# Feature buffer laid out feature by feature, and ten and nine features looked up instead of eight and seven

## Chip, cores and metric

The kernel runs on one core of one Trainium2 chip. Its time is device microseconds of one launch; the median of three runs stands below. Everything is float32.

## The reference

A recommendation model for 2048 examples: 26 embedding rows of 128 numbers are looked up for each, all pairs of the 27 vectors (26 features and the dense one) are multiplied, and a network of three layers runs on the result.

```python
e = jnp.stack([tbl_0[ids[:, 0]], ..., tbl_25[ids[:, 25]]], axis=1)      # (2048, 26, 128)
sd = jnp.einsum('bfd,bd->bf', e, dense)
ss = jnp.einsum('bfd,bgd->bfg', e, e)
z = jnp.concatenate([dense, sd, ss[:, iu, ju]], axis=1)                 # pairs iu < ju
h = jnp.concatenate([z, dense], axis=1)
h = jnp.maximum(h @ W_top1 + b_top1, 0.0)                               # 607 x 512
h = jnp.maximum(h @ W_top2 + b_top2, 0.0)                               # 512 x 256
y = h @ W_top3                                                          # 256 x 1
```

Ten of the tables have 1000 rows, which is the smallest size; the others have 1250, 12500 or 125000.

## The kernel before

The examples are worked on in eight chunks of 256, numbered by `(h, par)`, chunk `2h + par`. A feature reaches `feat`, the buffer [128 numbers, chunk parity, ...] from which the dot products are made, in one of two ways.

*Gathered.* GpSimd issues two indirect DMAs for a feature and chunk (L374), 128 rows each, into `rows`. TensorE transposes them through `tr_ps` (L573), ScalarE copies the result to `feat` (L412). Features go in units of two or one; the buffer of a unit is free for the next chunk when its transposes are done (`transposed`).

*Looked up.* For the first eight (`par` 0) or seven (`par` 1) of the small tables, the whole table lies in SBUF as a high and a low part. VectorE compares the ids of the chunk with the row numbers (eight comparisons a feature, L515), and TensorE multiplies the two parts with the result (16 matmuls, L588, into `oh_ps`); ScalarE copies to `feat` (L418). At the start each table is loaded by SyncE, split by ScalarE (`table_hi`, L391) and VectorE (`table_lo`, L502).

The dot products of a chunk come in eight steps of 8 groups (L606): each matmul takes one position of the chunk, two examples at once, and two of them run on the two halves of the array's columns. In `feat`, laid out `[QS, Q, FS]`, the 27 features of an example stand side by side, padded to 32. So TensorE reads neighbouring numbers, 59 for the weights and 52 for the moving side, and ScalarE writes feature by feature, 512 bytes apart. ScalarE (L427) and VectorE (L525) copy the products to `dots`, SyncE stores them to DRAM (L288) and loads them again in another order as `zt` (L299, L302). Layer 1 is L628, layer 2 L639, layer 3 L647.

A float32 matmul stands as two instructions in the profile, so a chunk has 256 matmul rows at L606.

The order on TensorE and ScalarE is written out by hand. In `SLOT`, `d` is a step of dot products of the finished chunk, `i` a shift of ids, `r` a unit of transposes of the next chunk, `l` a lookup, `f` the copy of the dense features, `m` a step of the network (`m0` to `m3` layer 1, `m4` layer 2, `m5` layer 3). One slot is run for each chunk. In the last slots, layers of the last two chunks are put behind the last transposes and dot products:

```python
SLOT_BEFORE_LAST = SLOT[0].replace(" m4", "").replace(" m5", "")
SLOT_LAST = "r0 d0 r1 d1 r2 d2 r3 d3 r4 d4 r5 d5 r6 d6 f r7 d7"
...
run("m4 r8 m5 r9", rows=(last, 1), done=(last - 1, 1))
run(DOTS, done=(last, 1))
run(MLP, done=(last, 0))
run(MLP, done=(last, 1))
```

Of the kernel before, what the change touches and what calls it, by code (L numbers as in the profile page):

```python
# [8 lines left out]
N1, N2 = 512, 256  # L9
# [4 lines left out]
LOOKUPS = (8, 7)  # L14
# [18 lines left out]
def units(fs):  # L33
# [8 lines left out]
FS = 32  # L42
# [60 lines left out]
def dlrm_tower(nc, dense_t, idx, ids_t, tables, w1, b1, w2, b2, w3, y):  # L103
    fp32, fp32r, i32 = mybir.dt.float32, mybir.dt.float32r, mybir.dt.int32
# [5 lines left out]
    with ctx:  # L110
# [9 lines left out]
        feat = sb("feat", [P, 2, QS, Q, FS], fp32)  # L120
# [3 lines left out]
        ids_bc = sb("ids_bc", [P, NO, CH], i32)  # L124
        rows = sb("rows", [P, NR, TILES, D], fp32)
        dense_sb = sb("dense_sb", [P, CH], fp32)
# [9 lines left out]
        h2 = sb("h2", [P, CH], fp32)  # L136
# [4 lines left out]
        ids_local = ids_bc[:].bitcast(fp32)  # L141
# [6 lines left out]
        feat1 = feat[:, 1].rearrange("p g q f -> p (g q f)")  # L148

        def raw_table(u):  # L150
            if u == 0:
                return dots[:, 0:RPP * D]
            if u == NO - 1:
                return zt[:].rearrange("p c b -> p (c b)")
            return feat1[:, (u - 1) * RPP * D:u * RPP * D]
# [568 lines left out]
```

## Time and profile before

| | |
|---|---|
| median of three runs | 423.53 us (423.44 to 424.53) |
| the profiled execution | 424.92 us |
| its span, first to last instruction | 422.8 us |
| TensorE matmul busy | 344.4 us (81%) |
| ScalarE busy | 198.8 us (47%) |
| VectorE busy | 163.0 us (39%) |
| GpSimd busy | 288.1 us (68%) |
| TensorE's granted clock, mean | 0.91 of full speed |

Busy times come from the profiled execution, and shares are of its span. TensorE's busy time is in wall time: at half clock the same work counts double. A timeline row merges like instructions that follow one another: start, length from the first start to the last end, number, and in brackets the idle time before them with what ended it. Instructions of TensorE overlap, so the step from one start to the next is what a burst costs, and not its own length. L numbers are lines of the kernel.

### The profile page before, as it was taken

The numbers are of one execution on the slowest core, as the hardware profiler recorded it, in microseconds if no ns is written. First come the engines' busy times: TensorE is split into PE (matmuls) and PEld (weight loads), VectorE is DVE, ScalarE is ACT, GpSimd is POOL, SyncE is SP. The second block draws the span as 40 slices with busy tenths as digits, with TensorE's granted clock in tenths as the row PEclk, the third lists the DMA queues.
The fourth block names the chain that finished last, engine by engine and source line by source line (L and its number), as shares of the span: only waits on it lengthen the run. The fifth ranks groups of instructions, "written<-read, shape, count | busy, mean of one in ns | idle before, by whom it ended". The sixth has DMA issues, their size and how long they took to land.

```text
span 422.8 us, 9641 instructions
## 1 busy us (share of the span) xinstructions
PE 344.4 (81%) x3752; PEld 311.6 (74%) x3752; DVE 163.0 (39%) x556; ACT 198.8 (47%) x302; POOL 288.1 (68%) x302
## 2 busy tenths in 40 slices
PE   1889869888896998698798999698996755579987
PEld 1879859878795797687697789697885544468876
DVE  5789538510754029510285029510781011112100
ACT  3478555435743455444554466443853422234312
POOL 5777777777777777777777777777777777770000
PEclk9999998899988999989899999889999955559989
DMA  7994573642255223542246424632253222224310
GB/s 173 265 237 110 138 218 95 159 131 52 59 143 185 55 55 87 157 130 53 61 95 160 130 55 96 183 93 53 59 140 88 55 52 55 52 58 122 70 46 2
DMA packets 45240, 44.66 MB, mean 106 GB/s; under 512 B 30415, under 2 KB 36807, under 8 KB 45198
## 3 DMA queue, kind: packets, MB, share of 16 engines
q1 hardware_dynamic: 35726, 24.63, 21.9%
q0 software_dynamic: 9472, 19.42, 17.7%
q8 instruction: 33, 0.54, 0.5%
q14 instruction: 9, 0.07, 0.0%
HBM read 38.26 MB, written 5.76 MB: 104 GB/s over the span
## 4 chain that ended last, share of the span: by engine, by line
POOL 61%; issue 20%; PE 10%; DMA 6%; SPq 1%; POOLq 1%; ACT 0%; DVE 0%
POOL rows L374 61%; DMA rows<-tbl_dram,idx_sb 4%; PE mlp_ps L628 3%; PE mlp_ps L639 3%; PE dot_ps L606 2%; PE tr_ps L573 1%; DMA dots_scratch<-rows 1%; SPq L288 1%; DMA zt<-dots_scratch 1%; SPq L299 1%; PE mlp_ps L647 1%; DMA idx_sb<-idx_dram 0%; POOLq L369 0%; POOLq L110 0%; POOLq L370 0%
## 5 line engine op out<-in xcount | busy, mean ns | idle before, releaser
L374 POOL DMA_INDIRECT rows<-tbl_dram,idx_sb x296 | 287.6, 971 | 92.2 <-issue 87.8
L515 DVE TENSOR_SCALAR onehot<-ids_bc 125x256 fp32r<-125x256 f32 x480 | 113.4, 305 | 41.3 <-PE oh_ps L588 31.6
L412 ACT ACTIVATE feat<-tr_ps 128x512 f32<-128x512 f32 (+1 forms) x80 | 81.4, 1017 | 58.8 <-PE tr_ps L573 57.7
L525 DVE COPY dots<-dot_ps 59x416 f32<-59x416 f32 x56 | 33.3, 594 | 177.1 <-PE dot_ps L606 158.6
L573 PE MATMUL tr_ps<-ident,rows 128*128 128x128 f32 x296 | 52.9, 302 | 51.1 <-DMA rows<-tbl_dram,idx_sb 50.8
L588 PE MATMUL oh_ps<-onehot,table_hi 125*128 125x256 f32 x480 | 77.3, 308 | 13.5 <-ACT table_hi L391 9.4
L573 PEld LDWEIGHTS tr_ps<-ident,rows 128*128 128x128 f32 x296 | 35.3, 151 | 63.2 <-DMA rows<-tbl_dram,idx_sb 37.0
L606 PE MATMUL dot_ps<-feat 128*59 128x52 f32 x2048 | 72.6, 234 | 7.9 <-issue 3.3
L588 PEld LDWEIGHTS oh_ps<-onehot,table_hi 125*128 125x128 f32 x480 | 67.1, 207 | 15.6 <-ACT table_hi L391 11.0
L606 PEld LDWEIGHTS dot_ps<-feat 128*59 128x59 f32 x2048 | 67.8, 150 | 14.4 <-issue 9.5
L588 PE MATMUL oh_ps<-onehot,table_lo 125*128 125x256 f32 x480 | 72.9, 299 | 0.0
L588 PEld LDWEIGHTS oh_ps<-onehot,table_lo 125*128 125x128 f32 x480 | 67.1, 207 | 0.5
L418 ACT ACTIVATE feat<-oh_ps 128x256 f32<-128x256 f32 x60 | 37.4, 623 | 62.0 <-PE oh_ps L588 60.4
L628 PE MATMUL mlp_ps<-zt,w_sb 117*128 117x256 f32 (+1 forms) x256 | 64.0, 400 | 2.5 <-DMA zt<-dots_scratch 2.5
L628 PEld LDWEIGHTS mlp_ps<-zt,w_sb 117*128 117x128 f32 (+1 forms) x256 | 49.5, 201 | 9.3 <-DMA zt<-dots_scratch 2.8
L427 ACT ACTIVATE dots<-dot_ps 59x416 f32<-59x416 f32 x56 | 27.9, 510 | 23.3 <-PE dot_ps L606 22.5
L434 ACT ACTIVATE h<-mlp_ps,b_sb 128x256 f32<-128x256 f32 x32 | 15.2, 474 | 38.3 <-PE mlp_ps L628 38.3
L639 PE MATMUL mlp_ps<-h,w_sb 128*128 128x256 f32 x128 | 30.5, 394 | 0.0
L639 PEld LDWEIGHTS mlp_ps<-h,w_sb 128*128 128x128 f32 x128 | 25.3, 199 | 3.7
L399 ACT ACTIVATE ids_bc<-ids_bc,row_f 128x768 f32<-128x768 int32 (+2 forms) x24 | 19.5, 818 | 6.0 <-DMA ids_bc<-ids_t_dram 6.0
L439 ACT ACTIVATE h<-mlp_ps,b_sb 128x256 f32<-128x256 f32 x16 | 7.6, 473 | 21.1 <-PE mlp_ps L639 21.1
L647 PEld LDWEIGHTS mlp_ps<-w_sb,h 128*128 128x128 f32 x64 | 7.8, 192 | 2.3 <-ACT h L439 2.3
(23 smaller groups left out, 47.1 us busy)
## 6 DMA issues: line engine op xcount, KB each, us to landing
dots_scratch<-dots SPq DMA_DIRECT2D x28, 175.5 KB
rows<-tbl_dram,idx_sb POOLq DMA_INDIRECT x296, 2.6
ids_bc<-ids_t_dram SPq DMA_DIRECT2D x12, 384.0 KB, 4.2
feat<-tbl_dram SPq DMA_DIRECT2D x6, 480.0 KB
ids_bc<-ids_t_dram SPq DMA_DIRECT2D x4, 512.0 KB, 5.3
zt<-dots_scratch SPq DMA_DIRECT2D x16, 117.0 KB
ids_bc<-ids_t_dram SPq DMA_DIRECT2D x8, 128.0 KB, 4.2
dense_sb<-dense_t_dram SPq DMA_DIRECT2D x8, 128.0 KB
```

Source lines behind the costliest of these rows:

```text
L374: nc.gpsimd.indirect_dma_start(rows[:, g, t, :], None, tables[UNIT[par][u][k]], bass.IndirectOffsetOnAxis(ap=idx_sb[:, par, g * TILES + t: ...
L399: nc.scalar.activation(ids_local[:, a:b, :], ids_bc[:, a:b, :], ACT.Identity, bias=row_f[:, 0:1]).then_inc(ids_shifted, 1)
L412: nc.scalar.activation(feat_view(par, fs[0] + 1, m, max(step, 1)), tr_ps[:, 0:m].rearrange("p f (q g) -> p f q g", q=Q), ACT.Copy).then_in ...
L418: nc.scalar.activation(feat_view(par, ONEHOT[u] + 1, 1, 1)[:, 0], lookup_psum(u).rearrange("p (q g) -> p q g", q=Q), ACT.Copy).then_inc(lo ...
L427: nc.scalar.activation(*dot_copy(h, par, v, 0), ACT.Copy).then_inc(dots_out_act, 1)
L515: last = nc.vector.tensor_scalar(onehot[0:TP, lookup_place(u), c, :], ids_local[0:TP, u, :], float(c), None, ALU.is_equal)
L525: nc.vector.tensor_copy(*dot_copy(h, par, v, 1)).then_inc(dots_out_dve, 1)
L573: last = nc.tensor.transpose(tr_ps[:, k, t * P:(t + 1) * P], rows[:, 2 * u + k, t, :], ident[:])
L588: last = nc.tensor.matmul(lookup_psum(u), part[0:TP, u, c * D:(c + 1) * D], onehot[0:TP, lookup_place(u), c, :], start=(part is table_hi a ...
L606: last = nc.tensor.matmul(dot_ps[dot_rows(t), v % 2, gi * PACK * NJ:(gi + 1) * PACK * NJ], batches.rearrange("p q f -> p (q f)")[:, 0:FS * ...
L628: last = nc.tensor.matmul(mlp_ps[:, x % 2, 0:CH], w1_sb[0:m, c, x * P:(x + 1) * P], zt[0:m, c, :], start=(c == 0), stop=(c == ZC))
L639: last = nc.tensor.matmul(mlp_ps[:, x, 0:CH], w2_sb[:, c, x * P:(x + 1) * P], h1[:, c, :], start=(c == 0), stop=(c == N1 // P - 1))
```

## The change

Seven things are altered together.

- `feat` becomes `[P, 2, NF, CH]`: a feature's 256 examples lie side by side. ScalarE writes neighbouring numbers; a matmul of the dot products reads one number of each feature and half chunk, 128 numbers (512 bytes) apart, 54 for the weights and 52 for the moving side. The padding and its memsets go. The examples of a chunk are put in another order (`grouped`) on the way in, so that one step serves both.
- Ten and nine features are looked up instead of eight and seven. 16 and 17 are gathered instead of 18 and 19: 264 gathers instead of 296, nine units instead of ten.
- The dense features are loaded straight into `feat`, already in the new order; ScalarE's copy `f` and `dense_sb` go. TensorE waits for `dense_loaded`.
- The ids are int16 instead of int32, in SBUF and in DRAM; the shift is made in place in int16.
- The second layer's output lies in `zt` (before, in `h2` and `h1`), and `zt` is loaded again only after layer 3 of the chunk before (`l3_done`, not `l1_done`).
- The products of the two examples of a matmul stand in alternate partitions, and the four stores read them so.
- The written orders are new. Layers 1 to 3 of the chunk before the last stand within the last slot, and only the last chunk's network follows the last dot products.

```diff
-LOOKUPS = (8, 7)
+LOOKUPS = (10, 9)
...
-START = ["i0 s0 s1 i1 l0 s2 l1 s3 i2 l2 s4 l3 s5 r0 l4 s6 l5",
-         "s7 r1 i0 i1 l6 r2 l7 r3 f",
-         "l0 i2 r4 l1 r5 l2 l3 r6 l4 r7 l5 r8 l6 r9"]
...
+START = ["i0 s0 s1 i1 s2 l0 s3 l1 r0 i2 s4 l2 s5 l3 r1 s6 l4 s7 l5 r2 s8 l6 s9 l7 r3",
+         "l8 i0 l9 i1 r4 r5",
+         "l0 i2 l1 r6 l2 l3 l4 r7 l5 l6 r8 l7 l8"]
...
+SLOT = ["d0 i0 d1 i1 d2 i2 d3 r0 d4 d5 d6 d7 r1 l0 l1 r2 l2 l3 r3 l4 l5 r4 m0 m1 r5 m2 l6 r6 m3 l7 r7 m4 l8 r8 m5",
+        "d0 i0 d1 i1 d2 i2 d3 r0 d4 d5 d6 d7 r1 l0 l1 r2 l2 l3 r3 l4 l5 r4 l6 m0 r5 m1 m2 l7 r6 m3 l8 r7 m4 l9 r8 m5"]
...
+SLOT_LAST = "r0 d0 d1 d2 d3 r1 d4 d5 d6 d7 r2 r3 r4 m0 r5 m1 r6 m2 m3 r7 m4 m5 r8"
...
-        feat = sb("feat", [P, 2, QS, Q, FS], fp32)
+        feat = sb("feat", [P, 2, NF, CH], fp32)
...
-        ids_bc = sb("ids_bc", [P, NO, CH], i32)
+        ids_bc = sb("ids_bc", [P, NO, CH], i16)
...
         def feat_view(par, f0, nf, step):
-
-            v = feat[:, par].rearrange("p g q f -> p f q g")
-            return v[:, f0:f0 + step * (nf - 1) + 1:step]
+            return feat[:, par, f0:f0 + step * (nf - 1) + 1:step, :]
...
             def next_dense(h, par):
 
-                sp.wait_ge(dense_out, chunk(h, par) + 1)
+                sp.wait_ge(dots_done, GUNITS * chunk(h, par))
                 load_dense(*following(h, par))
...
-                    own = dots_of(h, par)[FS * q:FS * q + NI].rearrange("p (k j g) -> p k j g", k=PACK, j=NJ)
-                    sp.dma_start(products[:, :, q * QS:(q + 1) * QS], own[:, q % PACK]).then_inc(dots_stored, DMA)
+                    t, k = divmod(q, PACK)
+                    own = dots_of(h, par)[TILE * t + k:TILE * t + k + PACK * (NI - 1) + 1:PACK]
+                    sp.dma_start(products[:, :, q * QS:(q + 1) * QS],
+                                 own.rearrange("p (j k g) -> p j k g", k=PACK, j=NJ)[:, :, k]
+                                 ).then_inc(dots_stored, DMA)
                 if not (isinstance(n, int) and n == 0):
 
-                    sp.wait_ge(l1_done, N1 // P * n)
+                    sp.wait_ge(l3_done, n)
...
-                        batches = feat[:, par, v * GPU + gi, t * PACK:(t + 1) * PACK]
+                        batches = feat[:, par].rearrange("p f (k b) -> p (f k) b", k=PACK)[:, :, t * QS + v * GPU + gi]
                         last = nc.tensor.matmul(dot_ps[dot_rows(t), v % 2, gi * PACK * NJ:(gi + 1) * PACK * NJ],
-                                                batches.rearrange("p q f -> p (q f)")[:, 0:FS * (PACK - 1) + NI],
-                                                batches[:, :, 0:NJ],
+                                                batches, batches[:, 0:NJ * PACK],
                                                 start=True, stop=True)
...
-            run("m4 r8 m5 r9", rows=(last, 1), done=(last - 1, 1))
             run(DOTS, done=(last, 1))
-            run(MLP, done=(last, 0))
             run(MLP, done=(last, 1))
...
+    def grouped(a):
+
+        return a.reshape(Q // PACK, PACK, QS, -1).transpose(1, 0, 2, 3).reshape(CH, -1)
```

## Rows read from the trace of the kernel before

**Rows 1.** The page's first part: busy time of the engines, share, instructions.
```profile
PE 344.4 (81%) x3752; PEld 311.6 (74%) x3752; DVE 163.0 (39%) x556; ACT 198.8 (47%) x302; POOL 288.1 (68%) x302
```

**Rows 2.** The page's fourth part: the chain that ended last, by engine.
```profile
POOL 61%; issue 20%; PE 10%; DMA 6%; SPq 1%; POOLq 1%; ACT 0%; DVE 0%
```

**Rows 3.** The waits: who waited for whom, us, times, longest.
```profile
POOL rows L374 <- issue: 87.8, 288, 0.3
...
PE tr_ps L573 <- DMA rows<-tbl_dram,idx_sb: 50.8, 33, 3.5
...
PE mlp_ps L628 <- DMA zt<-dots_scratch: 2.5, 2, 2.0
...
POOL rows L374 <- PE tr_ps L573: 2.1, 7, 0.3
```

**Rows 4.** Timeline of GpSimd: first and last of 296 gathers (start, us).
```profile
3.47 1.10 POOL L374 DMA_INDIRECT rows<-tbl_dram,idx_sb  x1 [2.31 <-DMA idx_sb<-idx_dram]
...
379.98 0.94 POOL L374 DMA_INDIRECT rows<-tbl_dram,idx_sb  x1 [0.30 <-issue]
```

**Rows 5.** Timeline of TensorE: where chunks 0, 1 and 7 begin their dot products.
```profile
55.23 4.84 PE L606 MATMUL dot_ps<-feat 128*59 128x52 f32 x160 [0.74 <-issue]
...
105.16 1.04 PE L606 MATMUL dot_ps<-feat 128*59 128x52 f32 x31 [1.09 <-ACT feat L412]
...
385.85 6.83 PE L606 MATMUL dot_ps<-feat 128*59 128x52 f32 x230 [0.69 <-ACT feat L412]
```

**Rows 6.** Busy time by stretch, the six slots (length, engines, clock, DMA).
```profile
105.20:385.80 280.60, 229.60 (x2630) 206.66 (x2630) 99.16 (x344) 132.27 (x201) 209.29 (x219) 0.88 0.36 94
```

**Rows 7.** Timeline of TensorE, 221 to 248 us, bursts without a wait.
```profile
221.75 1.12 PE L588 MATMUL oh_ps<-onehot,table_hi 125*128 125x256 f32 x8
...
223.67 0.60 PE L573 MATMUL tr_ps<-ident,rows 128*128 128x128 f32 x4
224.03 1.21 PE L588 MATMUL oh_ps<-onehot,table_hi 125*128 125x256 f32 x8
...
239.56 1.90 PE L628 MATMUL mlp_ps<-zt,w_sb 117*128 117x256 f32 x8
241.29 3.62 PE L639 MATMUL mlp_ps<-h,w_sb 128*128 128x256 f32 x16
244.75 0.38 PE L573 MATMUL tr_ps<-ident,rows 128*128 128x128 f32 x2
...
246.88 0.95 PE L647 MATMUL mlp_ps<-w_sb,h 128*128 128x1 f32 x8
```

**Rows 8.** ScalarE's groups by form: busy us, mean ns, idle before.
```profile
L412 ACT ACTIVATE feat<-tr_ps 128x512 f32<-128x512 f32 x68 | 73.9, 1087 | 57.8 <-PE tr_ps L573 56.9
...
L427 ACT ACTIVATE dots<-dot_ps 59x416 f32<-59x416 f32 x56 | 27.9, 510 | 23.3 <-PE dot_ps L606 22.5 <-issue 0.8
...
L399 ACT ACTIVATE ids_bc<-ids_bc,row_f 128x768 f32<-128x768 int32 x12 | 11.1, 926 | 0.6 <-DMA ids_bc<-ids_t_dram 0.6
...
L412 ACT ACTIVATE feat<-tr_ps 128x256 f32<-128x256 f32 x12 | 7.4, 618 | 1.0 <-PE tr_ps L573 0.7
...
L399 ACT ACTIVATE ids_bc<-ids_bc,row_f 128x1024 f32<-128x1024 int32 x4 | 4.6, 1144 | 1.4 <-DMA ids_bc<-ids_t_dram 1.4
```

**Rows 9.** Timeline of VectorE at the start: tables, then chunk 1's comparisons.
```profile
31.51 1.81 DVE L515 TENSOR_SCALAR onehot<-ids_bc 125x256 fp32r<-125x256 f32 x8
...
34.38 3.67 DVE L515 TENSOR_SCALAR onehot<-ids_bc 125x256 fp32r<-125x256 f32 x16
...
47.76 1.94 DVE L515 TENSOR_SCALAR onehot<-ids_bc 125x256 fp32r<-125x256 f32 x8 [0.44 <-PE oh_ps L588]
```

**Rows 10.** Timeline of TensorE in the tail.
```profile
393.03 0.96 PE L606 MATMUL dot_ps<-feat 128*59 128x52 f32 x26 [0.36 <-issue]
393.92 7.19 PE L628 MATMUL mlp_ps<-zt,w_sb 117*128 117x256 f32 x32
...
406.77 8.87 PE L628 MATMUL mlp_ps<-zt,w_sb 117*128 117x256 f32 x32 [0.59 <-DMA zt<-dots_scratch]
```

More of the change, by code:

```diff
@@ L100, with dlrm_tower @@
 Z_DMAS = ZC + 2
-def dlrm_tower(nc, dense_t, idx, ids_t, tables, w1, b1, w2, b2, w3, y):
-    fp32, fp32r, i32 = mybir.dt.float32, mybir.dt.float32r, mybir.dt.int32
+def dlrm_tower(nc, dense_t, dense_f, idx, ids_t, tables, w1, b1, w2, b2, w3, y):
+    fp32, fp32r, i32, i16 = mybir.dt.float32, mybir.dt.float32r, mybir.dt.int32, mybir.dt.int16
     ACT = mybir.ActivationFunctionType
@@ L140, in dlrm_tower @@
         ident = sb("ident", [P, P], fp32)
-        ids_local = ids_bc[:].bitcast(fp32)
         diag = h1[:, 2, 0:P].bitcast(i32)
         w1_dense2 = h1[:, 0:2, :].rearrange("p a b -> p (a b)")
-        feat1 = feat[:, 1].rearrange("p g q f -> p (g q f)")
         def raw_table(u):
-            if u == 0:
-                return dots[:, 0:RPP * D]
             if u == NO - 1:
                 return zt[:].rearrange("p c b -> p (c b)")
-            return feat1[:, (u - 1) * RPP * D:u * RPP * D]
+            home, slot = (dots[:], u) if u < 3 else (feat[:, 1].rearrange("p f b -> p (f b)"), u - 3)
+            return home[:, slot * RPP * D:(slot + 1) * RPP * D]
         tr_ps = ps("tr_ps", [P, 2, CH], fp32)
@@ L253, in load_dense @@
             def load_dense(h, par):
-                sp.dma_start(dense_sb[:], dense_t[bass.ds(chunk(h, par), 1)].rearrange("a p b -> (a p) b")
+                sp.dma_start(feat[:, par, 0, :], dense_f[bass.ds(chunk(h, par), 1)].rearrange("a p b -> (a p) b")
                              ).then_inc(dense_loaded, DMA)
@@ L465, in run @@
                         transposed_to_feat(*rows, x)
-                    if kind == "f":
-                        dense_to_feat(*rows)
                     if kind == "l":
@@ L484, in _ @@
             last = NCH // 2 - 1
-            run(SLOT_BEFORE_LAST, rows=(last, 0), done=(last - 1, 1), look=(last, 1))
+            run(SLOT[0], rows=(last, 0), done=(last - 1, 1), look=(last, 1))
             run(SLOT_LAST, rows=(last, 1), done=(last, 0))
-            run("m4 r8 m5 r9", rows=(last, 1), done=(last - 1, 1))
             run(DOTS, done=(last, 1))
-            run(MLP, done=(last, 0))
             run(MLP, done=(last, 1))
@@ L679, in _ @@
             last = NCH // 2 - 1
-            run(SLOT_BEFORE_LAST, rows=(last, 0), done=(last - 1, 1), look=(last, 1))
+            run(SLOT[0], rows=(last, 0), done=(last - 1, 1), look=(last, 1))
             run(SLOT_LAST, rows=(last, 1), done=(last, 0))
-            run("m4 r8 m5 r9", rows=(last, 1), done=(last - 1, 1))
             run(DOTS, done=(last, 1))
-            run(MLP, done=(last, 0))
             run(MLP, done=(last, 1))
@@ L695 @@
     dense = np.asarray(inputs["r_dense_features"])
+    ids16 = ids.view(np.int16).reshape(B, F, -1)[:, :, 0]
+    def grouped(a):
+        return a.reshape(Q // PACK, PACK, QS, -1).transpose(1, 0, 2, 3).reshape(CH, -1)
     idx = np.zeros((NCH, P, NR, TILES), ids.dtype)
@@ L700 @@
         for u, fs in enumerate(UNIT[n % 2]):
-            unit_ids = ids[n * CH:(n + 1) * CH, fs].reshape(TILES, P, len(fs))
+            unit_ids = grouped(ids[n * CH:(n + 1) * CH, fs]).reshape(TILES, P, len(fs))
             idx[n, :, 2 * u:2 * u + len(fs)] = unit_ids.transpose(1, 2, 0)
@@ L708 @@
         "idx": idx.reshape(NCH, P, NR * TILES),
-        "ids_t": ids[:, ONEHOT].reshape(NCH, CH, NO).transpose(0, 2, 1),
+        "dense_f": np.stack([grouped(dense[n * CH:(n + 1) * CH]).T for n in range(NCH)]),
+        "ids_t": np.stack([grouped(ids16[n * CH:(n + 1) * CH, ONEHOT]).T for n in range(NCH)]),
     }
@@ L719 @@
     y = nc.dram_tensor("y_dram", (P, B // P), mybir.dt.float32, kind="ExternalOutput").ap()
-    dlrm_tower(nc, aps["dense_t"], aps["idx"], aps["ids_t"], [aps[f"tbl_{f}"] for f in range(F)],
+    dlrm_tower(nc, aps["dense_t"], aps["dense_f"], aps["idx"], aps["ids_t"], [aps[f"tbl_{f}"] for f in range(F)],
                aps["W_top1"], aps["b_top1"], aps["W_top2"], aps["b_top2"], aps["W_top3"], y)
```

39 lines of the change are left out of this document (9 added, 30 removed).

## The prediction

> **What bounds the kernel now.** I began with the totals of the engines, where TensorE leads by far [rows 1], and then read the chain of waits, which says otherwise: followed back from the end, most of the time is GpSimd's gathers, with the gaps between them called issue [rows 2]. The waits say what those gaps are [rows 3]: 0.3 us after nearly every gather, and a wait for TensorE only 2.1 us in all. So GpSimd's queue runs without a pause from its first gather to its last [rows 4]: 3.47 to 380.92 us for 296 gathers, 1.275 us each. TensorE waits for it, 50.8 us in all, at the transposes [rows 3]. The timeline of the dot products says the same [rows 5]: chunk 1's begin at 105.16 us, chunk 7's at 385.85, six slots of 46.8 us, and 222 gathers in six slots (37 a slot) at 1.263 us make 46.7. What follows the last gather is a tail: transposes, then 37.0 us from 385.85 to the end of the span at 422.8.
>
> How close is TensorE to being the next bound? Over those six slots it is busy 229.6 of 280.6 us, with its clock at the lower of its two levels, 1.2 of 2.4 GHz, for part of it (mean 0.88) [rows 6]. Full-speed prices come from bursts with no wait in them: a lookup (16 matmuls) 1.92 us, the same with the change of tile about 1.96; four transposes 0.36 to 0.44 us, about 0.11 each; layer 1 1.73 us for one of its four steps, layer 2 3.46, layer 3 0.9 [rows 7]; the dot products 6.83 us for 230 starts, 29.7 ns each [rows 5], so 7.6 us for the 256 of a chunk and about 8.1 with one short wait for a copy. A slot of before: 8.1 + 7.5 x 1.96 + 37 x 0.11 + 11.3 = 38.2 us. GpSimd has 46.7. The difference is what there is to win.
>
> **The change, part by part.** *Fewer gathers.* 33 a slot instead of 37: 33 x 1.263 = 41.7 us. GpSimd gives up 5.0 us a slot.
>
> *More lookups, fewer transposes on TensorE.* Two lookups more, +3.9 us; four transposes fewer, -0.45 us.
>
> *The dot products read feat 512 bytes apart.* The stationary side falls from 59 columns to 54, the moving side stays at 52. The trace has no TensorE read with a large step, so the price has to be bounded. The nearest rows are ScalarE's, which is the engine that pays for the layout today: it writes feat 512 bytes apart. Its 128x512 form takes 1087 ns and the 128x256 form 618, so 1.83 ns an element; its contiguous in-place shift takes 1144 ns for 1024 and 926 for 768, 0.85 ns an element [rows 8]. A write with the large step costs 0.98 ns an element more. But the copy of dot_ps reads PSUM 208 bytes apart and takes 510 ns for 416 elements, 1.23 ns each with its fixed part in it [rows 8]: a read with a large step shows no such surcharge. Each pair of matmul instructions (both column tiles run side by side) takes 59.4 ns. Transposes and lookups load 128 columns of weights in 110 and 120 ns, 0.86 and 0.94 ns a column, and 59 columns at that pace are 51 to 55 ns of the 59.4: loading weights seems to be what sets the pace, at a rate no higher than ScalarE's. Lower bound: the read costs nothing and five columns fewer save 4.5 ns a pair, 0.6 us a chunk. Upper bound: ScalarE's surcharge on 54 weight columns, 53 ns a pair, +6.8 us a chunk; if the moving side paid it too, and not alongside, twice that. I take the lower, because the operation is a read, the row nearest to it in kind (PSUM) is free, and TensorE already asks for only about one element in 0.9 ns. Dot products: 7.5 us a chunk with their waits.
>
> The Trainium skill, page "SBUF — State Buffer", section "Specifications (TRN2)", speaks against this choice: SBUF is read in lines of 16 bytes, full bandwidth needs at least two accesses to a line, and every step to a new line pays. The page does not say how much; by it the sum would be that of the first rival, and no row here shows it for a TensorE read.
>
> *ScalarE.* Its copies into feat become contiguous: 0.98 x 512 = 0.5 us less for a pair of features, 0.25 less for one; over a slot of about 7.5 pairs and 11 single ones 6.5 us less. The copy of dense_sb goes (0.7 us). ScalarE is not on the path; what is won is that transposes and dot products wait less for it, some tenths a slot. It is hidden behind TensorE's own work.
>
> *SyncE.* Dense features go straight to feat; the same bytes, an earlier permission. The four stores of dot products keep runs of 256 bytes. The ids halve in bytes. What is new is that layer 3 must be done before the next zt is loaded (its second-layer output lives there); layer 3 ends a slot, the load comes some 8 us into the next, so this costs nothing inside the loop.
>
> *VectorE.* 9.5 sets of 8 comparisons instead of 7.5: +3.7 us of a slot in which it is idle for more than half. A set (1.8 us and 0.3 of handing over) fits behind one lookup with a transposition between; I allow 0.3 us a slot.
>
> *A slot, then:* 7.5 + 9.5 x 1.96 + 33 x 0.11 + 11.3 = 41.0 us of TensorE against 41.7 of GpSimd. They nearly meet. On top, layer 1 comes 21 us into a slot, and z was ready 12.8 us after the last dot product in the tail [rows 10], which is 20.8 to 21.5 us into it and later when gathers share the queues: 1.5 us (before, all chunks together waited 2.5 us for it [rows 3]). With VectorE's 0.3 and half a dozen small waits for copies I take 43.7 us a slot.
>
> *The start gets longer.* Each table passes through VectorE (comparisons, then the low part) at one in 2.87 us, without a pause; after the eighth, at 34.38, come chunk 1's sets, seven in 15.3 us, done at 49.70 [rows 9]. Two tables more end at 40.1, nine sets at 2.19 us at 59.8; the last lookup and its copy make 62. Before, the first dot products began at 55.23 [rows 5], held by gathers; these now end some 5 us sooner and do not matter. So +6.8 us here. Two more tables of 0.5 MB load in the same time; I give this no price, since VectorE comes to them only after 34 us.
>
> *The end.* The slot of chunk 6 has no lookups now or before, and layer 1 to 3 of that chunk now stand inside it, ahead of the last transposes. Dot products and transposes to 8.6 us, 13 us for z, then 11.3 + 1.6 (transposes) + 1 (waits for relu) + 3 (clock: the engine has stood still, and the same 32 matmuls took 8.87 us after a wait and 7.19 without [rows 10]) + 0.8 = 39.4 us. By then the gathers are done, before layer 1 can begin: 3.5 + 264 x 1.275 = 340 us, against 62 + 6 x 43.7 + 21.6 = 346. The tail was 37.0 us; its wait for z is no longer filled with the chunk before, so more of the last layers runs at half clock: 38.0.
>
> *Sum:* 62.0 + 6 x 43.7 + 39.4 + 38.0 = 401.6 us of span. The profiled execution took 424.92 us with a span of 422.8, 2.1 outside; the median is 423.53, 1.4 below it. Forecast: 401.6 + 2.1 - 1.4 = 402.3, given as **402 us**.
>
> **The rivals.** *The step costs what ScalarE's does (slower).* Place: every dot product's weights. Price: 53 ns a pair, 128 pairs, 6.8 us a chunk, none of it hidden, as TensorE is then the only bound. 402 + 8 x 6.8 = 456 us. It decides from (423.5 - 402) / 8 = 2.7 us a chunk, 21 ns a pair, 0.39 ns a column. For it: the only SBUF access with this step in the trace pays 0.98 ns an element. Against: that is a write. The 16-byte lines of the Trainium skill's page "SBUF — State Buffer", section "Specifications (TRN2)", would be this case.
>
> *Less is won: start and waits.* Tables late, z later among the gathers (3 us a slot instead of 1.5), or gathers that grow to 1.35 us beside more comparisons (assumed): 33 x 1.35 = 44.6 us a slot. 1 to 3 us a slot, 408 to 421.
>
> *No gain.* The dot products take about 2.7 us a chunk more, a part of the surcharge: 422 to 425.
>
> *GpSimd stays the bound.* It would be at 41.7 us a slot, and that is below the forecast's 43.7, so it can't make the kernel slower than forecast at today's pace; it is the floor: 402 - 6 x 2 = 390. It has no chance of its own, being the lower end of the forecast's.
>
> **How the numbers follow.** Forecast 0.66, its own range 391 to 408; less won 0.13; no gain 0.03; the step's full price 0.18. The range leaves out the last, which stands alone far away: 391 to 424. For this kernel 0.3%, 1.3 us, is about what a measurement can tell from no change. Faster 0.79, same 0.03, slower 0.18.
>
> **What would show it.** The dot products' burst of 32 at 0.9 us or less at full clock, weight loads of 54 columns in about 125 ns, means the read is free; 1.6 us means the rival. GpSimd waiting for transposes, and TensorE hardly for gathers, shows that the bound has moved. Dot products of chunk 0 should begin near 62 us, and the six slots after it take 43 to 45 us. ScalarE's 128x512 copy should be near 600 ns, the 128x256 copy near 380. The prediction is wrong if the dot products are slower than some 10 us a chunk (7.5 + 2.7); if lookups wait for VectorE by more than a microsecond a slot; or if the last slot waits for z longer than 13 us.

## The result, and the profile after

The changed kernel takes 562.59 us (median of four, 562.2 to 562.9), the kernel before 424.03 us beside it: a ratio of 1.327 (1.324 to 1.329), 138.6 us slower. The forecast was 402 us in 391 to 424. The profiled execution took 562.2 us with a span of 559.9. Of all kernels below, ratios leave out single executions over 1.5% above the fastest of the same kernel, and medians keep them.

The page of the changed kernel, its totals and, further down, the chain that ended last:

```profile
PE 497.4 (89%) x3976; PEld 470.1 (84%) x3976; DVE 309.8 (55%) x684; ACT 287.8 (51%) x304; POOL 292.1 (52%) x270
...
PE 53%; DMA 13%; DVE 10%; ACT 8%; issue 8%; SPq 7%; ACTq 0%; DVEq 0%
```

The bound has moved from GpSimd to TensorE, as forecast, but TensorE, VectorE and ScalarE all have far more busy time than in [rows 1]: 153, 147 and 89 us. The work that was added is far less than that. The groups by form (busy us, mean ns of one, idle before) say where they sit:

```profile
L364 POOL DMA_INDIRECT rows<-tbl_dram,idx_sb x264 | 291.6, 1104 | 163.9 <-PE tr_ps L549 86.5 <-issue 74.7 <-DMA idx_sb<-idx_dram 2.8
L582 PE MATMUL dot_ps<-feat 128*54 128x52 f32 x2048 | 207.7, 400 | 11.4 <-ACT dots L409 5.1 <-DVE dots L501 2.6 <-issue 1.9
...
L491 DVE TENSOR_SCALAR onehot<-ids_bc 125x256 fp32r<-125x256 int16 x608 | 175.0, 400 | 67.4 <-PE oh_ps L564 56.8 <-ACT ids_bc L389 8.9
L501 DVE COPY dots<-dot_ps 54x416 f32<-54x416 f32 x56 | 118.5, 2128 | 104.0 <-PE dot_ps L582 102.7
L409 ACT ACTIVATE dots<-dot_ps 54x416 f32<-54x416 f32 x56 | 113.0, 2035 | 23.7 <-PE dot_ps L582 23.0
...
L396 ACT ACTIVATE feat<-tr_ps 128x512 f32<-128x512 f32 x60 | 59.1, 985 | 8.3 <-PE tr_ps L549 6.4
...
L389 ACT ACTIVATE ids_bc<-ids_bc,row_f 128x768 int16<-128x768 int16 x8 | 21.4, 2671 | 0.0
...
L501 DVE COPY rows<-dot_ps 54x416 f32<-54x416 f32 x8 | 4.8, 594 | 47.8 <-PE dot_ps L582 47.8
...
L409 ACT ACTIVATE rows<-dot_ps 54x416 f32<-54x416 f32 x8 | 4.1, 511 | 19.2 <-PE dot_ps L582 19.2
```

Three things are to be seen. The dot products, whose matmul took 234 ns on the mean before, take 400. The copies of their result to `dots` take 2.0 us on ScalarE instead of 0.51 [rows 8], and 2.1 on VectorE, while the same copies to `rows` (the last chunk's) keep their 0.51 and 0.59: same form, another place in SBUF. And operations that have nothing to do with the layout have grown too: a 128x768 shift of ids from 926 ns to 2671, the gathers from 971 ns to 1104, the comparisons from 305 to 400. ScalarE's 128x512 copy, which should have fallen from 1087 to about 600, took 985.

The timeline of chunk 3's dot products shows who grows with whom (start, length, idle before):

```profile
264.11 6.84 PE L582 MATMUL dot_ps<-feat 128*54 128x52 f32 x64 [0.26 <-DVE dots L501]
264.20 3.33 ACT L409 ACTIVATE dots<-dot_ps 54x416 f32<-54x416 f32 x1
267.42 3.49 ACT L389 ACTIVATE ids_bc<-ids_bc,row_f 128x768 int16<-128x768 int16 x1
...
270.80 0.52 ACT L409 ACTIVATE dots<-dot_ps 54x416 f32<-54x416 f32 x1
...
271.92 3.34 PE L582 MATMUL dot_ps<-feat 128*54 128x52 f32 x32
```

A burst of 32 (one step of dot products) lasts 3.34 us, 104 ns an instruction against 29.7 before [rows 5]. A copy or a shift that starts beside a burst ends when the burst ends (264.20 to 267.53, 267.42 to 270.91); the copy at 270.80, between two bursts, takes 0.52. Where the copies go to `rows`, TensorE is quicker as well, 22.72 us for 256, 88.8 ns each (the gathers have ended by then too, so that these rows alone do not say which of the two it is; experiment 13 does):

```profile
508.34 22.72 PE L582 MATMUL dot_ps<-feat 128*54 128x52 f32 x256 [0.47 <-ACT feat L396]
511.75 0.51 ACT L409 ACTIVATE rows<-dot_ps 54x416 f32<-54x416 f32 x1 [3.46 <-PE dot_ps L582]
```

The waits, beside [rows 3]: GpSimd, which had waited 2.1 us for TensorE, now waits 86.5, and the waits for z are 29.4.

```profile
POOL rows L364 <- PE tr_ps L549: 86.5, 22, 14.9
...
PE mlp_ps L603 <- DMA zt<-dots_scratch: 29.4, 6, 12.9
```

The busy time from chunk 0's dot products to the last chunk's, the six slots and the last one (length, TensorE, its weight loads, VectorE, ScalarE, GpSimd, clock, DMA), beside the 280.6 us of [rows 6] for the six alone:

```profile
62.40:508.30 445.90, 414.93 (x3329) 392.58 (x3328) 259.02 (x513) 252.69 (x244) 245.88 (x221) 0.84 0.25 66
```

Chunk 0's dot products begin at 62.4 (forecast 62.0), the six slots take 63.4 to 66.9 us (43.7), the last 57.7 (39.4), and 51.5 us follow (38.0). In a slot the dot products with the transposes between them now last about 28 us (257.6 to 286.2 for chunk 3).

### The profile page after: what moved, and what is told of

The parts are those of the page before. It is cut to its first block, busy times and chain, and to the rows that moved or that the text cites. A ratio compares the mean times of both kernels' runs of the same rounds, so it can differ in the third digit from the quotient of the medians.

```text
span 559.9 us, 10201 instructions
## 1 busy us (share of the span) xinstructions
PE 497.4 (89%) x3976; PEld 470.1 (84%) x3976; DVE 309.8 (55%) x684; ACT 287.8 (51%) x304; POOL 292.1 (52%) x270
## 4 chain that ended last, share of the span: by engine, by line
PE 53%; DMA 13%; DVE 10%; ACT 8%; issue 8%; SPq 7%; ACTq 0%; DVEq 0%
PE dot_ps L582 17%; PE oh_ps L564 15%; PE mlp_ps L603 11%; DVE onehot L491 6%; ACT dots L409 5%; PE mlp_ps L614 5%; DMA dots_scratch<-dots 5%; DMA feat<-tbl_dram 4%; PE tr_ps L549 4%; DVE dots L501 3%; DMA zt<-dots_scratch 3%; SPq L277 3%; SPq L290 2%; ACT ids_bc L389 2%; PE mlp_ps L622 1%
## 5 line engine op out<-in xcount | busy, mean ns | idle before, releaser
L364 POOL DMA_INDIRECT rows<-tbl_dram,idx_sb x264 | 291.6, 1104 | 163.9 <-PE tr_ps L549 86.5
L582 PE MATMUL dot_ps<-feat 128*54 128x52 f32 x2048 | 207.7, 400 | 11.4 <-ACT dots L409 5.1
L582 PEld LDWEIGHTS dot_ps<-feat 128*54 128x54 f32 x2048 | 200.2, 305 | 19.4 <-ACT dots L409 14.2
L491 DVE TENSOR_SCALAR onehot<-ids_bc 125x256 fp32r<-125x256 int16 x608 | 175.0, 400 | 67.4 <-PE oh_ps L564 56.8
L501 DVE COPY dots<-dot_ps 54x416 f32<-54x416 f32 x56 | 118.5, 2128 | 104.0 <-PE dot_ps L582 102.7
L409 ACT ACTIVATE dots<-dot_ps 54x416 f32<-54x416 f32 x56 | 113.0, 2035 | 23.7 <-PE dot_ps L582 23.0
L564 PE MATMUL oh_ps<-onehot,table_hi 125*128 125x256 f32 x608 | 97.0, 305 | 15.5 <-ACT table_hi L381 10.6
L564 PEld LDWEIGHTS oh_ps<-onehot,table_hi 125*128 125x128 f32 x608 | 83.8, 202 | 18.9 <-ACT table_hi L381 11.2
L603 PE MATMUL mlp_ps<-zt,w_sb 117*128 117x256 f32 (+1 forms) x256 | 64.8, 406 | 29.4 <-DMA zt<-dots_scratch 29.4
L564 PE MATMUL oh_ps<-onehot,table_lo 125*128 125x256 f32 x608 | 87.8, 288 | 0.0
L396 ACT ACTIVATE feat<-tr_ps 128x512 f32<-128x512 f32 (+1 forms) x72 | 63.6, 884 | 8.4 <-PE tr_ps L549 6.4
L389 ACT ACTIVATE ids_bc<-ids_bc,row_f 128x256 int16<-128x256 int16 (+3 forms) x24 | 53.2, 2215 | 5.0 <-DMA ids_bc<-ids_t_dram 5.0
```

Source lines behind the costliest of these rows:

```text
L364: nc.gpsimd.indirect_dma_start(rows[:, g, t, :], None, tables[UNIT[par][u][k]], bass.IndirectOffsetOnAxis(ap=idx_sb[:, par, g * TILES + t: ...
L389: nc.scalar.activation(ids_bc[:, a:b, :], ids_bc[:, a:b, :], ACT.Identity, bias=row_f[:, 0:1]).then_inc(ids_shifted, 1)
L396: nc.scalar.activation(feat_view(par, fs[0] + 1, m, max(step, 1)), tr_ps[:, 0:m], ACT.Copy).then_inc(transposed_out, 1)
L409: nc.scalar.activation(*dot_copy(h, par, v, 0), ACT.Copy).then_inc(dots_out_act, 1)
L491: last = nc.vector.tensor_scalar(onehot[0:TP, lookup_place(u), c, :], ids_bc[0:TP, u, :], float(c), None, ALU.is_equal)
L501: nc.vector.tensor_copy(*dot_copy(h, par, v, 1)).then_inc(dots_out_dve, 1)
```

## The experiments

Three explanations are to be told apart: TensorE pays for each number that lies in new 16 bytes (the line); 512 bytes is a bad distance as such (the distance); the copies are held up because of where `dots` lies relative to what TensorE reads (the place of `dots`). In the first eight experiments every variant of the kernel, that of before too, took 100 to 150 us more than it did later, with pauses on all engines that the profile puts down to another core or an unknown queue (22% of the chain in experiment 1); what caused them is not known, and those times are compared only with the one beside them. The kernels were then run again where the kernel before took 424 us, and the accounts below rest on these. A pair is two instructions of TensorE that run side by side, one on each column tile; a chunk has 128 pairs.

**1, 6 and 10: the whole change, but TensorE reads neighbouring numbers.** They are not the numbers that a dot product needs, so this kernel's output is not the reference's; it only shows what the addresses cost.

```diff
-                        batches = feat[:, par].rearrange("p f (k b) -> p (f k) b", k=PACK)[:, :, t * QS + v * GPU + gi]
+                        at = (t * QS + v * GPU + gi) * NF * PACK
+                        batches = feat[:, par].rearrange("p f b -> p (f b)")[:, at:at + NF * PACK]
```

> The changed kernel, but each matmul of the dot products reads 54 and 52 numbers that stand side by side in the feature buffer (other numbers than it should, so the products are not the reference's); counts, orders, lookups and all else as in the change. Theory: the 512-byte step is the whole of the loss; the burst of 32 falls from 3.35 us to 0.9, the copies of the dot products to 510 and 594 ns, and the kernel takes about the 402 us that I had forecast (395 to 410). Rival: ten and nine lookups and the missing cover in the last slot cost too; then it stays over 424 us.

> The same program as in the first experiment, on another chip, as there every kernel, the one before included, took some 130 us more than it had with idle stretches in all engines. The changed kernel reading neighbouring numbers (the wrong ones): about 402 us if the step of the read is all that my sum missed.

> The changed kernel reading neighbouring numbers (the wrong ones), where the kernel before takes 424 us. Beside a kernel before of 551 and 562 us it took 0.97 of it. If the step of the reads is the whole of what my sum missed: 395 to 410 us, a little less than the version with 27 features side by side (410), since ScalarE's copies are short here.

Measured: 536.76 beside 550.93 (ratio 0.974, 0.970 to 0.978), 543.88 beside 561.96 (0.973, 0.966 to 0.979), and 411.19 beside 424.51 (0.969, 0.963 to 0.975). The groups of the last:

```profile
L364 POOL DMA_INDIRECT rows<-tbl_dram,idx_sb x264 | 259.7, 984 | 82.3 <-issue 77.7 <-PE tr_ps L549 2.4 <-DMA idx_sb<-idx_dram 2.2
L491 DVE TENSOR_SCALAR onehot<-ids_bc 125x256 fp32r<-125x256 int16 x608 | 142.0, 303 | 73.1 <-PE oh_ps L564 62.1 <-ACT ids_bc L389 9.2 <-issue 0.5
L583 PE MATMUL dot_ps<-feat 128*54 128x52 f32 x2048 | 62.8, 220 | 8.7 <-issue 4.7 <-DVE dots L501 1.9 <-ACT dots L409 1.0
...
L396 ACT ACTIVATE feat<-tr_ps 128x512 f32<-128x512 f32 x60 | 35.8, 597 | 5.6 <-PE tr_ps L549 3.4
```

Nothing but the addresses of one read separates this from 562.6 us, and with them the gathers (984 ns), comparisons (303), copies (508 on ScalarE) and shifts (925) all go back to their old durations, or nearly. So the read costs 151.4 us (562.6 - 411.2), what it does to the other engines included, and the rest of the change is worth 13.3 us (424.5 - 411.2). I had expected 395 to 410 us.

**2, 7 and 11: 528 bytes instead of 512.** Four unused numbers behind each half of a feature. The buffers behind `feat` lie 1728 bytes further by it; nothing else differs.

```diff
-        feat = sb("feat", [P, 2, NF, CH], fp32)
+        feat = sb("feat", [P, 2, NF, PACK, HP], fp32)     # HP = 132; views take [..., 0:CH // PACK]
```

> The changed kernel with four numbers of padding behind each half feature, so that TensorE reads 528 bytes apart instead of 512; correct products. Theory A (numbers a multiple of 256 or 512 bytes apart come out of the same place of a partition's memory, and everything that wants that place queues for it): the burst of 32 drops to 0.9 to 1.2 us and the copies to 510 to 600 ns; about 400 to 415 us in all. Theory B (every number that is not next to the last one costs its own access, whatever the step): the burst stays at 3.3 us and the time within 2% of 562.6 us.

> The same program as in the second experiment, again on another chip; correct products, step of 528 bytes. From the bursts of the fourth experiment: a pair costs about 100 ns instead of 59 (4 bytes) and 190 (512 bytes), and ScalarE's copies beside it are free. So +41 ns x 128 pairs = 5.3 us a chunk against the 402: 440 to 455 us, slower than before, faster than the change. If the first rule held alone (a step costs nothing unless it is a multiple of 256) it would be 402 to 415.

> The changed kernel with a step of 528 bytes, correct products, where the kernel before takes 424 us. A pair at about 100 ns instead of 54 to 59: +41 to 46 ns x 128 = 5.3 to 5.9 us a chunk, 8 chunks, on top of some 400 us of the version that reads neighbours: 440 to 450 us.

Measured: 560.26 (1.019, 1.012 to 1.027), 569.39 (1.012, 1.006 to 1.018), and 440.64 (1.039, 1.034 to 1.045). From the last:

```profile
L583 PE MATMUL dot_ps<-feat 128*54 128x52 f32 x2048 | 107.5, 284 | 3.2 <-issue 2.6 <-ACT feat L397 0.5
...
L502 DVE COPY dots<-dot_ps 54x416 f32<-54x416 f32 x56 | 33.3, 595 | 109.9 <-PE dot_ps L583 109.1
...
208.70 6.71 PE L583 MATMUL dot_ps<-feat 128*54 128x52 f32 x128 [2.40 <-issue]
...
215.92 6.75 PE L583 MATMUL dot_ps<-feat 128*54 128x52 f32 x128
```

Every number still lies in 16 bytes of its own. The dot products are busy 107.5 us instead of 62.8, 105 ns a pair instead of 61 (2 x 107.5 / 2048), and the kernel pays 29.4 us for it (440.6 against 411.2). It is less than the 44.7 us of busy time because TensorE's other matmuls are busy 9.4 us less (385.6 - 107.5 against 350.3 - 62.8) and it stands still 10 us less in the profiled executions, whose spans are 25.2 us apart. One gain shows in the timeline: the 128 instructions after the wait ran at a granted clock of 0.50 and then 0.64, and the next 128 at 1.00, and both took 6.7 us, while with neighbouring numbers the lower clock costs 4.84 us against 3.63 (below). The other 122 us (562.6 - 440.6) are gone, and so is the growth of every other engine. The line explains a fifth (29.4 of 151.4); the rest goes with a distance of 512, and 528 does not have it.

**3 and 13: `dots` moved by 96 bytes, distance 512 kept.**

```diff
+        sb("gap", [P, 24], fp32)
         dots = sb("dots", [P, PACK * NJ * QS], fp32)
```

> The changed kernel with 96 bytes of unused memory in front of dots, so that each copied product lands 96 bytes further on. In the change, the copies of a step write addresses that are equal mod 256 to those that TensorE reads at that moment (feature buffer from byte 16512, dots from 192928), and take 3.5 us; those of the last chunk go to rows (from 175232), 32 bytes lower mod 256, and take 0.51 us. Theory A (places by low address bits): copies that run beside a burst fall to 0.51 and 0.59 us in all chunks; TensorE's burst stays near 3 us; id shifts and comparisons, which touch all addresses, stay slow. Theory B: copies stay at 3.5 us, since then what differs in the last chunk is that gathers have ended.

> The changed kernel with 96 bytes in front of dots, where the kernel before takes 424 us. In the third experiment the copies of the dot products fell to 0.57 and 0.59 us and the burst stayed slow. If the hold-up of these copies is what the change loses besides the reads themselves: 562 us falls by the 0.2 to 0.6 us that TensorE waits at each of 56 steps, some 15 to 30 us, to 530 to 550. If it is only a symptom beside TensorE's own slow reads: 555 to 563.

Measured: 628.2 (one run) beside 550.93, and 526.98 beside 423.47 (1.244, 1.239 to 1.249). From the last:

```profile
L365 POOL DMA_INDIRECT rows<-tbl_dram,idx_sb x264 | 289.7, 1097 | 132.9 <-issue 75.4 <-PE tr_ps L550 55.0 <-DMA idx_sb<-idx_dram 2.5
L583 PE MATMUL dot_ps<-feat 128*54 128x52 f32 x2048 | 188.9, 385 | 3.8 <-issue 2.1 <-ACT dots L410 0.7 <-ACT feat L397 0.5
...
L502 DVE COPY dots<-dot_ps 54x416 f32<-54x416 f32 x56 | 33.3, 594 | 158.2 <-PE dot_ps L583 157.9
...
256.64 11.48 PE L583 MATMUL dot_ps<-feat 128*54 128x52 f32 x128
257.53 1.62 POOL L365 DMA_INDIRECT rows<-tbl_dram,idx_sb  x1 [12.10 <-PE tr_ps L550]
```

In the change `feat` begins at byte 16512 of a partition and `dots` at 192928. Step v of the dot products reads numbers whose address leaves 128 + 32v on division by 256, and the copies of step v - 1, which run beside it, write to 160 + 32(v - 1), the same; those to `rows` (175232) lie 32 bytes lower. The place of `dots` matters: 96 bytes give VectorE's copies their 594 ns back and the kernel 35.6 us (562.6 - 527.0). TensorE gains too: 89.7 ns an instruction in the middle of the kernel (11.48 / 128), beside comparisons and gathers, against 104. The mean of a dot product's matmul stays at 385 of 400 ns, and gathers (1097), comparisons (386) and shifts (2167) stay long although no copy to `dots` is held up any more, so it is not VectorE's long copies that hold the gathers up. I had expected 530 to 550 us.

**4: reads and writes by themselves.** This kernel makes bursts of 32 positions for both column tiles (64 matmuls on float32, so 64 pairs of instructions) on data of no meaning, at 18 distances, then parts of them, then ScalarE's copies beside them.

```python
STEPS = [(1, 64), (2, 64), (4, 64), (8, 64), (16, 64), (32, 64), (64, 64), (128, 64),       # numbers from one to
         (128, 8), (128, 4), (129, 64), (130, 64), (132, 64), (136, 64), (144, 64), ...]    # the next, between tiles
w = feat[:, a:a + ws * 53 + 1:ws]
m = feat[:, a:a + ms * 51 + 1:ms]
nc.tensor.matmul(dot_ps[64 * t:64 * t + 54, 0, 0:52], w, m, start=True, stop=True)
```

> A kernel of its own, that computes nothing of the reference: bursts of 32 pairs of the dot product's matmuls (54 and 52 columns, two column tiles), one for each step between the numbers from 4 to 1024 bytes; then with only weights or only the moving side at a large step; then one column tile alone; then ScalarE copying beside a burst, to addresses equal to TensorE's mod 256 or 4 to 128 bytes off. Theory A: a burst gets slower with each doubling of the step up to 256 or 512 bytes, stays slow at 1024, and is nearly free at 516, 528, 544 bytes; weights alone at 512 cost about half of what both cost; ScalarE's copy takes some 0.5 us except at offset 0. Theory B: from 16 bytes on all steps cost the same, 528 included.

In the timeline of ScalarE a small copy marks each burst's end; the idle time before it is the burst with its handing over. Distances of 8, 16, (32 and 64 not shown,) 128, 256 and 512 bytes, 512 with the two tiles 32 bytes apart, and 528:

```profile
42.25 0.17 ACT L54 ACTIVATE out<-dot_ps 54x2 f32<-54x2 f32 x1 [3.91 <-PE dot_ps L74]
49.24 0.17 ACT L54 ACTIVATE out<-dot_ps 54x2 f32<-54x2 f32 x1 [6.83 <-PE dot_ps L74]
...
73.15 0.17 ACT L54 ACTIVATE out<-dot_ps 54x2 f32<-54x2 f32 x1 [9.32 <-PE dot_ps L74]
85.70 0.17 ACT L54 ACTIVATE out<-dot_ps 54x2 f32<-54x2 f32 x1 [12.38 <-PE dot_ps L74]
98.34 0.17 ACT L54 ACTIVATE out<-dot_ps 54x2 f32<-54x2 f32 x1 [12.47 <-PE dot_ps L74]
106.52 0.17 ACT L54 ACTIVATE out<-dot_ps 54x2 f32<-54x2 f32 x1 [8.01 <-PE dot_ps L74]
...
136.08 0.17 ACT L54 ACTIVATE out<-dot_ps 54x2 f32<-54x2 f32 x1 [6.83 <-PE dot_ps L74]
...
243.41 23.92 ACT L63 ACTIVATE out<-cp_ps 54x416 f32<-54x416 f32 x2 [6.22 <-PE dot_ps L74]
...
316.56 1.12 ACT L63 ACTIVATE out<-cp_ps 54x416 f32<-54x416 f32 x2 [11.79 <-PE dot_ps L74]
...
405.83 1.06 ACT L63 ACTIVATE out<-cp_ps 54x416 f32<-54x416 f32 x2 [20.88 <-PE dot_ps L74]
```

Divided by 64 pairs:

| bytes from one number to the next | ns a pair |
|---|---|
| 8 | 61 |
| 16, 32, 64, 516, 520, 528, 544, 576 | 107 to 110 |
| 128, 640 | 146 |
| 256, 512, 768, 1024 | 193 to 195 |
| 512, tiles 32 or 16 bytes apart | 125, 126 |

There are two steps in it. One is at 16 bytes and is paid by any larger distance. The other repeats: distances that differ by 512 cost the same (64 and 576, 128 and 640, 256 and 768), and 256 costs what 512 does. Most of it is what one would see if SBUF had 16 places of 16 bytes by an address's remainder on 256, and engines had to queue at a place: a distance of 64 uses four places, 128 two, 256 and 512 one. It is a picture that fits, and not in all: at 516 bytes up to four numbers in turn lie at one place, and that costs no more than 528 (6.93 us against 6.83 for a burst). Neither theory of the expectation holds as it stands: 528 bytes are not nearly free, and not as slow as 512.

Two streams at one place are the larger part of it. One tile alone needs 6.73 us at 528 for its 64 instructions, and two tiles side by side 6.83 for 128; at 512 one alone needs 8.01, and two 12.47, or 8.01 again when they are 32 bytes apart.

The last three rows are two ScalarE copies each, written beside bursts: to TensorE's own place at a distance of 512, 23.92 us instead of 1.05; 16 bytes beside it, 1.12; at a distance of 528, 1.06. Offsets of 4 and 8 bytes gave 13.31 and 11.52; 32, 64 and 128 gave 1.05. So a place is no wider than 16 bytes, and ScalarE is held up at it while TensorE streams from it. That 16 bytes are enough through a whole burst is not shown, since both move over 32 bytes: TensorE reads four positions from the first 16 (about 1.6 us, from 12.47 / 32 a position), and both copies of the row at 16 bytes may have been over by then. Offsets of 32 and more are free of that.

**5 and 9: the change without its layout.** Lookups, orders (but for `f`), int16 ids and the rest as in the change; `feat` position by position with 27 numbers a position, the products stored as before, and ScalarE's copy of the dense features back.

```diff
-        feat = sb("feat", [P, 2, NF, CH], fp32)
+        feat = sb("feat", [P, 2, QS, Q, NF], fp32)
+        dense_sb = sb("dense_sb", [P, CH], fp32)
...
+                        batches = feat[:, par, v * GPU + gi, t * PACK:(t + 1) * PACK]
+                                                batches.rearrange("p q f -> p (q f)"), batches[:, :, 0:NJ],
```

> Ten and nine lookups, int16 ids and the new orders as in the change, but the feature buffer laid out position by position as before, with the 27 features of an example side by side and without the padding (the same 55,296 bytes a partition as in the change), so that TensorE reads 54 and 52 neighbouring numbers and ScalarE writes 432 bytes apart; the dense features go through a copy of ScalarE again; correct products. If the whole of the loss is the step of TensorE's reads and the rest of my sum was right: burst of 32 at 0.9 us, slots of 43 to 46 us, 400 to 412 us in all, faster than before. If lookups, start and last slot cost more than I reckoned: 415 to 425 us.

> The same program as the one with 27 features side by side, once more, to see it where the kernel before takes its 424 us and not 550 to 562 as beside the first eight experiments (there it took 0.975 of the kernel before). Expected as there: 400 to 412 us if only the step of TensorE's reads was wrong in my sum; 415 to 425 if start, lookups and last slot cost more than reckoned.

Measured: 547.09 beside 561.96 (0.975, 0.969 to 0.982), and 410.07 beside 424.2 (0.959, 0.955 to 0.964). This one beats both kernels. Its groups:

```profile
L405 ACT ACTIVATE feat<-tr_ps 128x512 f32<-128x512 f32 x60 | 69.6, 1160 | 4.1 <-PE tr_ps L560 3.5
L593 PE MATMUL dot_ps<-feat 128*54 128x52 f32 x2048 | 61.2, 217 | 11.0 <-issue 5.2 <-ACT dots L418 2.4 <-ACT feat L405 2.3
```

ScalarE pays as much as ever for its writes, now 432 bytes apart (1160 ns; 1087 at 512, so that for these writes 512 is no bad distance), and is busy 205.3 us against the 153.8 of experiment 10. The kernel is not slower for these 51.5 us within what can be told here: its single executions lie between 404.6 and 416.5 us, those of experiment 10 between 408.6 and 414.2. That surcharge is hidden, so the layout had next to nothing to win.

**8 and 12: the layout alone.** `LOOKUPS = (8, 7)` and the orders of before, without `f`; the rest as in the change.

> The layout of the change, its direct load of the dense features and its int16 ids, but eight and seven lookups in the order of before (without f; the layers of the chunk before the last stand at the end of the last slot, since zt must be free). Correct products. The dot products cost 22 to 28 us a chunk instead of 8: 424 + 8 x 14 to 20 = 535 to 585 us, so within 5% of the change, if the layout is the whole of the loss; if the two lookups more were to blame for a good part, it would be under 500.

> The layout of the change with eight and seven lookups and the order of before, where the kernel before takes 424 us. Dot products of 24 to 28 us a chunk instead of 8 to 10, and copies held up by them; 535 to 600 us. Beside a kernel before of 562 us it took 1.197 of it, which would be 508 us; if it is at or above the change's 562 us, the two lookups more did not lose anything.

Measured: 671.6 beside 561.96 (1.197, 1.188 to 1.206), and 521.2 beside 424.51 (1.224, 1.215 to 1.232). I had expected 535 to 600 of the second and missed.

```profile
L364 POOL DMA_INDIRECT rows<-tbl_dram,idx_sb x296 | 345.7, 1168 | 92.1 <-issue 87.8 <-DMA idx_sb<-idx_dram 2.2 <-PE tr_ps L549 2.1
L582 PE MATMUL dot_ps<-feat 128*54 128x52 f32 x2048 | 201.1, 395 | 6.8 <-ACT dots L409 3.1 <-issue 2.2 <-ACT feat L396 1.4
...
L409 ACT ACTIVATE dots<-dot_ps 54x416 f32<-54x416 f32 x56 | 31.3, 571 | 59.2 <-PE dot_ps L582 58.6
```

With fewer lookups GpSimd has no pause again, and its gathers, at 1168 ns, come to 345.7 + 87.8 us. The copies to `dots` are almost undisturbed: the gathers' index buffer ahead of `dots` takes 304 bytes instead of 272, and the other buffers ahead of it differ by multiples of 256, so `dots` lies 32 bytes beside the place that TensorE reads. So the 41.4 us between it and the change (562.6 - 521.2) are not the price of two lookups: moving `dots` was worth 35.6 us in experiment 13, and beside that kernel, which has `dots` out of the way too, this one is 5.8 us apart (527.0 - 521.2).

## Why the prediction was wrong

The account in times of undisturbed neighbours (before 423.5 to 424.5 in each): 411.2 with the neighbouring read; +29.4 for a new line with each number (440.6); +86.3 for a distance of 512, which puts all numbers at one place (527.0); +35.6 for `dots` at that place too (562.6).

- **The dot products read feat 512 bytes apart: the step that failed.** It was priced at nothing, with ScalarE's 53 ns a pair as the upper bound and twice that if the moving side paid as well. Measured at 528 bytes: 46 ns a pair more by itself (107 against 61), 44 in the kernel, which is 5.6 us a chunk of busy time and 3.7 us a chunk of the kernel's (29.4 / 8), within the 6.8 of the bound. Measured at 512: 134 more by itself (195 against 61), and in the middle of the kernel 209 a pair (3.34 us for 16) against 59.4. The choice rested on the row of PSUM copies, which is free at 208 bytes, and on TensorE's asking for only one number in 0.9 ns. PSUM is another memory: the row was near in kind of operation and far in what was accessed. (No run has ScalarE read SBUF with a large step, so that it is the memory, and not the engine, is argued.) The SBUF row, a write, gave nearly the right price for a new line: 1.83 ns an element for ScalarE, and 105 / 54 = 1.94 ns a column for one tile of TensorE at 528 in experiment 4 (6.73 us / 64 = 105). With experiment 11's 29.4 us the sum would have been 431.
- **The upper bound was no bound.** "If the moving side paid too, and not alongside, twice that" is 13.6 us a chunk and gives 402 + 8 x 13.6 = 511 us, still below the result. In fact the moving side pays alongside: at 528 bytes a burst takes 6.71 us with only the weights apart, 6.45 with only the moving side, 6.83 with both. The bound was one on a line's price and left out that two streams and other engines may want one place. Nothing in the profile before shows that; the bound should have said so.
- **"The step costs what ScalarE's does"** had the right sign and the right first mechanism and gave 456 us; with that mechanism alone the kernel took the 440.6 us of experiment 11, and what the rival leaves out, the place, is the larger part of the loss. It had a chance of 0.18. The Trainium skill, page "SBUF — State Buffer", section "Specifications (TRN2)", has a penalty for each step to a new line of 16 bytes, and experiment 4 agrees: 61 ns a pair at 8 bytes, 107 at 16. That 512 is worse than 528 it does not say.
- **Everything else costed at nothing or left the same** (gathers at 1.263 us, comparisons in 1.8 us a set, ids, copies out of PSUM) was right as long as TensorE does not stream from one place: gathers, comparisons and 128x512 copies take 984, 303 and 597 ns in experiment 10. In the change they took 1104, 400 and 985. An engine's durations were taken as its own. And the 128x256 copy, foreseen near 380 ns, takes 383 there.
- **The remaining sum held well, and would have erred by 9 us.** Two sums in it are off by little (the terms of the last slot add up to 39.3 and not 39.4; the floor is 390 and the range begins at 391). Experiment 10, median 411.2 against 402.3, in its profiled execution a span of 412.3 against 401.6: start 62.3 against 62.0; six slots 273.7 against 262; last slot 36.8 against 39.4; tail 39.4 against 38.0. The term that was short is the slot. Experiment 10's six slots (length, TensorE busy, and further on the granted clock):

```profile
62.30:336.00 273.70, 255.87 (x2989) 240.17 (x2988) 136.18 (x505) 106.30 (x220) 208.21 (x215) 0.97 0.39 102
```

  Without work TensorE is 17.8 us, 3.0 a slot against 2.7 allowed. Busy it is 42.6 a slot against 41.0 at full clock, and the mean clock of 0.97 gives most of the difference: 6% of the time at the lower of its levels, which by estimate loses 1.4 in 45.6 us. Waits, and bursts after them and without them, in its timeline:

```profile
200.43 4.84 PE L583 MATMUL dot_ps<-feat 128*54 128x52 f32 x128 [2.24 <-issue]
...
226.85 5.41 PE L604 MATMUL mlp_ps<-zt,w_sb 117*128 117x256 f32 x16 [2.33 <-DMA zt<-dots_scratch]
...
335.99 3.63 PE L583 MATMUL dot_ps<-feat 128*54 128x52 f32 x128
...
356.94 3.57 PE L604 MATMUL mlp_ps<-zt,w_sb 117*128 117x256 f32 x8 [9.79 <-DMA zt<-dots_scratch]
```

  The same 128 instructions take 4.84 us after a wait (clock 0.50 in the first 2.2 us, mean 0.72) and 3.63 without (clock 1.00). A price of the lower clock after waits belonged into the slot, as it stood in the last one. The wait for z in the last slot, 9.8 us, stayed under the 13 named.
- **"ScalarE: some tenths a slot"** for contiguous writes was right, at the most: experiment 9 has the old kind of write and is as fast.
- **The bound.** GpSimd did wait for transposes (86.5 us) in the change, for the wrong reason. In experiment 10, where the prediction's kernel ran, GpSimd issued without a pause up to 343 us (2.4 us of waits for TensorE) and TensorE never waited for gathers, which had been 50.8 us: its lead grows by 45.6 - 33 x 1.275 = 3.5 us a slot, and that the row buffers took that up is the likely reason. Of the two signs named, "GpSimd waiting for transposes" was ill chosen and "TensorE hardly for gathers" was the right one.

What stays open: how the 86.3 us divide between TensorE's own queue and what the other engines do to it was not measured apart. TensorE's busy time on dot products alone grows by 81.4 us from experiment 11 to 13. In the last chunk of experiment 13, where no gathers or comparisons run, 256 instructions take 22.62 us, 177 ns a pair against 105, and by that pace the own queue would be 73 us for all 1024 pairs (an estimate). A kernel whose two column tiles read from different places, which took 125 instead of 195 ns a pair in experiment 4, was not run. Why gathers grow, 984 to 1104 ns, is only argued: they are long where dot products run (1.62 us at 257.53 in experiment 13, 0.94 elsewhere). And the picture of sixteen places is drawn from times alone.

## What to carry to other kernels

Price a strided access by a row of the same memory, even if that row is a write and the new access a read; the row of PSUM said nothing of SBUF here. Where an SBUF distance is a multiple of 128 bytes, ask who else is at that place at the time, and pad (528 for 512 gave back 122 of 151 us here, for 16 bytes behind each half feature). And before a layout is turned around to make a cheap engine cheaper, look whether its surcharge is on the path: 51.5 us of ScalarE were hidden, so no layout could win them, and the rest of the change without it (experiment 9, 410 us) was as fast as the change with harmless reads (experiment 10, 411).

## What the runs showed of the hardware that was not expected

- SBUF answers to TensorE in steps: 61 ns a pair of 54-column loads with 52 columns moved at 8 bytes, 107 to 110 from 16 bytes on, 146 at 128 and 640, 193 to 195 at 256, 512, 768 and 1024.
- One side with the distance already costs: weights 4 bytes and moving 512 apart took 7.90 us for a burst, the reverse 8.27; with 528, 6.45 and 6.71, against 3.91 with both 8 bytes apart. The second side adds little at 528 (6.83) and much at 512 (12.47).
- Reads with a large distance run at the same pace at either level of TensorE's clock: 6.71 us for 128 instructions at a granted clock of 0.50 to 0.64, 6.75 at 1.00 (528 bytes, experiment 11). With neighbouring numbers 4.84 and 3.63 (experiment 10). That its busy time counts double at half clock does not hold for such reads.
- An engine can be held up by another's reads: a ScalarE copy of 0.51 us took 3.3 in the kernel and 11.7 to 12.1 beside a longer burst (two in 23.92 us), if it wrote to the bytes (of each 256) from which TensorE read; 32 bytes away it took no longer. TensorE loses too: 104 ns an instruction with the copies at its place, 88.8 with them 32 bytes away (last chunk) and 89.7 with them 96 bytes away (experiment 13).
- Moving one buffer by 96 bytes was worth 35.6 us of 562.6.
